# A fused graph layer on one core: x read twice from a host-made layout, edge lists read ready for use, the gate's first layer moved into the main loop, and all 49 key products moved behind the prologue

## The reference

```python
xn = layernorm(x)
# graph attention, 4 heads of 64
h = xn @ W; a_src, a_dst = <h, att_src>, <h, att_dst>
e = leaky_relu(a_src[src] + a_dst[dst], 0.2)
alpha = softmax of e over the edges of each dst
gnn = sigmoid(segment_sum(alpha * h[src], dst) + bias)
# linear attention, 8 heads of 32, with a gate
q, k, v = split(xn @ Wqkv); k = softmax(k, axis=nodes)
out = q @ (k^T v)
hgate = gelu((layernorm(xn) * ln_g + ln_b) @ Wg1 + bg1)
gate = sigmoid(hgate @ Wg2 + bg2)
x = x + gnn + (out * gate) @ Wproj + bproj
# a feed-forward layer on the 3124 nodes with the largest router weight
xn2 = layernorm(x); w = xn2 @ wr + br
x = x + xn2 + (where w is among the top) w * (gelu(xn2 @ w1 + b1) @ w2 + b2)
```

## Time and profile before

| | us |
|---|---|
| median of 3 runs | 1600.1 |
| lowest, highest | 1594.01, 1605.51 |
| span of the profiled execution, first to last instruction | 1323.1 |

### The profile page before, as it was taken

The page is one execution under the profiler, slowest core; times in us unless marked ns, Lnnn a source line. Parts: engine busy times, 40 slices in busy tenths (PEclk is TensorE's granted clock), DMA queues, the critical chain, the costliest instruction groups (busy, mean ns, idle before and its releaser), DMA issues.

```text
span 1323.1 us, 24146 instructions
## 1 busy us (share of the span) xinstructions
PE 1060.3 (80%) x5817; PEld 791.9 (60%) x5817; DVE 1018.3 (77%) x2596; ACT 516.7 (39%) x1155; POOL 854.3 (65%) x891
## 2 busy tenths in 40 slices
PE   5998857785687878878788787897877978779786
PEld 4674635553465566656666566675665766567565
DVE  6776365657788877888788887888878878888788
ACT  4462423212334434343353443434434334344421
POOL 0621656767777777777777777777777777777000
PEclk9999878886788889888898888988889888898889
DMA  9527556766666666666666666666666666665205
GB/s 269 136 72 141 155 184 179 191 178 166 161 173 166 164 160 165 176 158 166 169 162 174 165 161 176 158 171 164 164 173 161 168 164 166 175 164 151 68 1 195
DMA packets 165907, 212.04 MB, mean 160 GB/s; under 512 B 49524, under 2 KB 131252, under 8 KB 165704
## 3 DMA queue, kind: packets, MB, share of 16 engines
q0 software_dynamic: 39984, 110.94, 33.8%
q1 hardware_dynamic: 117570, 97.15, 25.6%
q10 hardware_dynamic: 8306, 3.41, 1.2%
HBM read 165.93 MB, written 45.46 MB: 160 GB/s over the span
## 4 chain that ended last, share of the span: by engine, by line
PE 50%; DVE 15%; issue 11%; ACT 7%; DMA 3%; SPq 1%; DVEq 1%; ACTq 0%; POOL 0%; POOLq 0%
PE bank L1922 15%; PE bank L1887 14%; PE bank L1859 6%; PE bank L1898 5%; ACT L1630 4%; PE bank L1838 3%; DVE hot L1272 2%; PE bank L1847 2%; PE bank L2009 2%; PE bank L1738 2%; DVE ring L1357 2%; DVE xnT L1552 1%; DVE late L1394 1%; DMA parts_d<-wout 1%; ACT bn L1630 1%
## 5 line engine op out<-in xcount | busy, mean ns | idle before, releaser
L774 POOL DMA_INDIRECT ring<-feat_d,idx x832 | 816.0, 981 | 285.8 <-issue 226.5
L1357 DVE TENSOR_TENSOR ring<-ring,bank 128x1024 f32<-128x1024 f32 x208 | 240.0, 1217 | 1.8 <-ACT bank L1620 1.8
L1922 PE MATMUL bank<-late,w_s 128*128 128x256 f32 x768 | 232.4, 463 | 0.4 <-ACT hT L1680 0.4
L1887 PE MATMUL bank<-ring,hot 128*64 128x265 f32 x1664 | 206.8, 401 | 13.3 <-DVE ring L1357 13.2
L1922 PEld LDWEIGHTS bank<-late,w_s 128*128 128x128 f32 x768 | 183.6, 243 | 36.0 <-ACT hT L1680 0.5
L1887 PEld LDWEIGHTS bank<-ring,hot 128*64 128x64 f32 x1664 | 120.0, 141 | 93.8 <-issue 34.2
L1859 PE MATMUL bank<-w_s,hT 128*128 128x256 f32 x720 | 171.0, 392 | 1.2 <-ACT hT L1705 1.2
L1838 PE MATMUL bank<-ident,lk 128*16 128x128 f32 x208 | 42.7, 345 | 161.3 <-DVE lk L1317 161.3
L1620 ACT ACTIVATE bank<-diff 128x64 f32<-128x64 f32 x52 | 11.8, 228 | 376.5 <-DVE diff L1341 362.4
L1859 PEld LDWEIGHTS bank<-w_s,hT 128*128 128x128 f32 x720 | 137.7, 196 | 20.9 <-ACT hT L1705 1.4
L1838 PEld LDWEIGHTS bank<-ident,lk 128*16 128x16 f32 x208 | 17.5, 103 | 177.8 <-DVE lk L1317 136.8
(11 more groups left out here) (284 smaller groups left out, 1611.0 us busy)
## 6 DMA issues: line engine op xcount, KB each, us to landing
parts_d<-zero SPq DMA_DIRECT2D x59, 265.0 KB, 4.0
parts_d<-wout SPq DMA_DIRECT2D x208, 66.2 KB
lists<-dloc_d SPq DMA_DIRECT2D x104, 128.0 KB
ring<-feat_d,idx POOLq DMA_INDIRECT x832
parts<-parts_d SPq DMA_DIRECT2D x49, 265.0 KB
big<-in_x SPq DMA_DIRECT2D x7, 896.0 KB, 11.1
three<-in_x SPq DMA_DIRECT2D x49, 128.0 KB, 3.0
out<-xnT SPq DMA_DIRECT2D x5, 896.0 KB, 4.2
```

Of the source, the lines that this page charges most:

```text
L774: pool.indirect_dma_start(out=ring[:, u * TI + q, 0:AW], out_offset=None, in_=feat_d, in_offset=bass.IndirectOffsetOnAxis(ap=idx[:, u, q:q ...
L1357: V.tensor_tensor(feats, feats, ex[:, g * TG:(g + 1) * TG, :].unsqueeze(3) .to_broadcast([P, TG, HEADS, HD]), ALU.mult).then_inc(S("scaled ...
L1887: mm = T.matmul(bank[2 + n][c * WIN:(c + 1) * WIN, 0:SW], hot[:, q, :], ring[:, u * TI + q, 0:SW], start=(j == 0), stop=(j == TG - 1))
L1922: mm = T.matmul(bank[6 + g][:, m % 2 * 2 * P:(m % 2 + 1) * 2 * P], w1_s[:, t, m * P:(m + 1) * P], xn2T[:, t, :], start=(t == 0), stop=(t = ...
```

## The change

- `x` is laid out by the host as [128, 49, 256], so that a partition's rows are contiguous, and comes in a second time as `xt`, already transposed. ACT's queue loads both (14 DMAs of 7 KB rows), and after them eight edge lists. The transposes of x and their copies are gone.
- The edge lists come in the layouts in which they are used. The list work on POOL, the 48 list transposes and their copies are gone; DVE does six passes of 832 or 1,024 columns over 128 (or 104) partitions.
- The roots are made in four groups (7, 14, 14, 14 tiles).
- The gate's first layer leaves the prologue: `wa_s` has 264 columns; L529, the Gelu of L621, the transposes, their copies and the stores to `hid_d` are gone. In the main loop PE does it a step ahead of the tile's `mixer` (`hidden_ahead`, before `first_sums`), DVE scales it by the root (`scale_hidden`, before `products`), ACT applies Gelu (`gate_hidden`, after `hidden`), and SP loads the root as a row (`load_scales`) in place of `hidT`.
- The target scores are scaled by ACT and no longer by DVE; the products rotate over four banks.
- EARLY goes from 23 to 0: all key products come in the main stretch.
- SP clears ten tiles of `parts_d` after the feature stores and no longer before them.

```diff
-    EARLY = 23
+    EARLY = 0
-WA = C + 2 * HEADS + GH
+WA = C + 2 * HEADS
+        GROUPS = [0, XC, 3 * XC, 5 * XC, NT]
+        prod_bank = lambda i: bank[(2, 3, 6, 7)[i % 4]]
             def _(sp):
...
+                for p in range(PAIRS):
+                    store(p)
...
+                for t in (NT, *range(CLEARED)):
+                    clear(t)
                 for u in range(SLOTS):
                     sp.wait_ge(S(f"feat_out{u}"), 16 * ((PAIRS + SLOTS - 1 - u) // SLOTS))
...
                 def evacuate(i):
-                    products = bank[2 + i % 2]
...
-                    V.tensor_scalar(adst_s[:, i, :], products[:, AW:AW + HEADS], rstd[:, i:i + 1], None, ALU.mult
-                                    ).then_inc(S("adst_made"), 1)
...
-                    V.scalar_tensor_tensor(sc[:, i % 2, 0:GH], products[:, gate_cols], rstd2[:, i:i + 1],
-                                           b1row[:, :], ALU.mult, ALU.add).then_inc(S("hid_asked"), 1)
...
             def _(act):
+                for n in range(7):
+                    part = slice(n * XC, (n + 1) * XC)
+                    act.dma_start(xnT[:, part, :], xt[:, part, :]).then_inc(S(f"x{n}_in"), 16)
+                    act.dma_start(big[:, part, :], x[:, part, :]).then_inc(S(f"x{n}_in"), 16)
+                for o, i in edge_lists:
+                    act.dma_start(o, i).then_inc(S("lists_in"), 16)
...
+                def products(i):
+                    pe.wait_ge(S(f"x{i // XC}_in"), 32)
+                    if i >= 4:
+                        pe.wait_ge(S("adst_made"), i - 3)
...
+                def load_scales(i, u):
+                    if not known_below(i, 2):
+                        sp.wait_ge(S("hidT_made"), i - 1)
+                    sp.dma_start(rrow[:, u, :], rstd_d[bass.ds(i, 1), :].to_broadcast([GH, P])
+                                 ).then_inc(S(f"scales_in{u}"), 16)
...
-                    sp.dma_start(x_pair[p % 5][:, 0:n, 0:C], x.rearrange("(t p) c -> p t c", p=P)[:, 2 * p:2 * p + n, :]
+                    sp.dma_start(x_pair[p % 5][:, 0:n, 0:C], x[:, 2 * p:2 * p + n, :]
...
+                def scale_hidden_from(hid, i, u):
+                    dve.wait_ge(S("hid_done"), i + 1)
+                    dve.wait_ge(S(f"scales_in{u}"), 8 * (i - u) + 16)
+                    V.tensor_tensor(rrow[:, u, :], hid, rrow[:, u, :], ALU.mult).then_inc(S("hid_scaled"), 1)
...
+                def gate_hidden(i, u):
+                    act.wait_ge(S("hid_scaled"), i + 1)
+                    if not known_below(i, 2):
+                        act.wait_ge(S("gate_done"), i - 1)
+                    A.activation(hidT[:, u, :], rrow[:, u, :], ACT.Gelu, bias=b1col[:, 0:1]).then_inc(S("hidT_made"), 1)
...
                 def last_tiles():
                     i = NT - 3
                     merge_exp(i + 1, (i + 1) % 2)
+                    gate_hidden(i + 1, (i + 1) % 2)
+                    gate_hidden(i + 2, i % 2)
                     inverse_root(i, i % 2)
...
+                def hidden_ahead(i, u):
+                    pe.wait_ge(S("sums_kept"), NB * (i + LAG_MERGE - 2) + 1)
+                    if not known_below(i, 1):
+                        pe.wait_ge(S("hid_scaled"), i)
+                    hidden_to(hid_ps[0], i)
...
+                def hidden_to(hid, i):
+                    for t in range(CT):
+                        mm = T.matmul(hid, wg1_s[:, t, :],
+                                      xnT[:, bass.ds(i, 1), t * P:(t + 1) * P].rearrange("p a c -> p (a c)"),
+                                      start=(t == 0), stop=(t == CT - 1))
+                    mm.then_inc(S("hid_done"), 1)
```

More of the change, by code:

```diff
@@ L378, in _ @@
                 for ahead, op in ((1, ALU.is_lt), (2, ALU.is_le)):
-                    then(pool.tensor_tensor(t[:, 0:NG - ahead], first[:, ahead:NG], last[:, 0:NG - ahead], ALU.subtract))
+                    then(pool.tensor_tensor(t[:, 0:NG - ahead], first_e[:, ahead:NG], last_e[:, 0:NG - ahead], ALU.subtract))
                     settle()
@@ L705, in _ @@
-                pe.wait_ge(S("xnT_kept"), TURNED)
-                pe.wait_ge(S("weights_ready"), 4 * CT)
-                def products(i, u):
-                    if i >= 2:
-                        pe.wait_ge(S("hid_asked"), i - 1)
-                    tile = xnT[:, i, :]
+                pe.wait_ge(S("weights_ready"), 2)
+                for t in range(CT):
+                    mm = T.matmul(bank[0][:, 0:WA], ones[:, :], wa_s[:, t, :], start=(t == 0), stop=(t == CT - 1))
+                mm.then_inc(S("columns_summed"), 1)
@@ new lines, in _ @@
+                for t in range(CT):
+                    mm = T.matmul(bank[0][:, 0:GH], ones[:, :], wg1_s[:, t, :], start=(t == 0), stop=(t == CT - 1))
+                mm.then_inc(S("columns_summed"), 1)
+                each(9, 37)
+                pe.wait_ge(S("roots_ready"), len(GROUPS) - 1)
+                pe.wait_ge(S("ident_made"), 1)
+                T.transpose(bank[1][0:NT, 0:P], roots[:, 1, :], ident[:, :]).then_inc(S("rows_turned"), 1)
+                pe.wait_ge(S("bad_asked"), 1)
@@ L1108, in load_node @@
                         sp.wait_ge(S("merged"), free)
-                        sp.wait_ge(S("gate_done"), free)
                     for n in range(2):
@@ L1725, in _ @@
                 sweep(act, EARLY, NT, 1, 0, key_tile)
-                steps(act, [EDGES(exps), MERGE(merge_exp), HALF(hidden), LOAD_MIXER(load_mixer), MAXIMUM(logarithms), CONTEXT(context), EDGES(keep_sums),
+                steps(act, [EDGES(exps), MERGE(merge_exp), HALF(hidden), MERGE(gate_hidden), LOAD_MIXER(load_mixer), MAXIMUM(logarithms), CONTEXT(context), EDGES(keep_sums),
                             SUM(inverse_root), MERGE(gates), TURN(keep_turned)])
@@ L2037, with lay_out, padded @@
 FAR = 1 << 20
+def lay_out(x, src, dst):
+    def padded(a, rows, value):
+        full = np.full((-(-a.shape[0] // rows) * rows, *a.shape[1:]), value, a.dtype)
+        full[:a.shape[0]] = a
+        return full
+    x, src, dst = padded(x, P, 0), padded(src, IE, 0), padded(dst, IE, FAR)
+    tiles = x.reshape(-1, P, CT, P)
+    groups = dst.reshape(-1, GE)
+    after = np.full_like(groups, FAR + 1)
+    after[:, :-1] = groups[:, 1:]
+    by_row = lambda a: a.reshape(-1, GI, P, TG).transpose(2, 0, 1, 3).reshape(P, -1)
+    by_run = lambda a: a.reshape(-1, NB, 2, P, TG).transpose(0, 2, 1, 4, 3)
+    first, last = groups[:, 0], groups[:, -1]
+    base = np.broadcast_to(first.reshape(-1, NB, 2, 1, 1), (first.size // GI, NB, 2, P, TG))
+    runs = by_run(groups).reshape(-1, 2 * GE)
+    f = np.float32
+    return {
+        "x": x.reshape(-1, P, C).transpose(1, 0, 2), "xt": tiles.transpose(3, 0, 2, 1).reshape(P, -1, C),
+        "src": src, "dst": dst, "srct": by_row(src),
+        "curt": by_row(groups).astype(f), "nxtt": by_row(after).astype(f),
+        "curn": groups.reshape(P, -1).astype(f), "nxtn": after.reshape(P, -1).astype(f),
+        "curp": runs.astype(f), "basep": by_run(base).reshape(len(runs), -1, P)[:, :, 0].astype(f),
+        "ends": np.stack([first, last]).astype(f), "first": first[None, :],
+    }
 def kernel(**inputs):
```

529 lines of the change are left out of this document (224 added, 305 removed).

## The result

The changed kernel took 1639.4 us in the median of four runs (1631.7 to 1656.4), the kernel before 1602.8 (1594.0 to 1609.9): a ratio of 1.022 (95% interval 1.016 to 1.028). So it is slower by over 1%. The ratio is taken round by round and leaves out the execution of 1656.4, which ran over 1.5% above the fastest. The forecast was 1594 (1568 to 1612) and no change.

What follows compares the result with a forecast made beforehand. It took PE to bound the prologue and a circle through PE, ACT and DVE the loop, not POOL's gathers. Terms -50 + 22 + 22 - 1 + 1 = -6 gave 1594 us, range 1568 to 1612.

Steps and rivals of the forecast that it cites:

- The base: Whole kernel: sum made against the profiled span of 1323.1 us, with 277 us up to the median carried over unchanged.
- ahead of the first scan -28 forecast: Stretch before the loop: 50 us gained in the prologue, 22 us lost in the key products.
- in the loop +21 forecast: Main loop: +22 us for PE's new records, -1 for x in the context sum, 0 for DVE, ACT and SP.
- Prologue, -50: Before the main stretch: DVE becomes the bound, with 61 us of work from 18 on; main stretch begins at 86.5, not 136.8.
- the sign that I had named for being wrong: Prologue: the prediction is wrong if DVE waits there for ACT's roots or for x.
- the rival with the DMA rate of 263: Prologue bound by its DMAs, 24 MB at 263 GB/s: gain only 38 us, time 1606; chance 0.14.
- Keys, +22: Start of the main stretch: 23 more key products at 0.954 us each, hidden by nothing, +22 us.
- PE in the loop, +22: Each step: four new PE records ahead of the window sums add 0.5 us to the circle in about 45 tiles.
- My rival: Loop: new PE work runs at the lower clock, 1.0 us a step, loop costs 45, time 1617; chance 0.12.
- SP, 0: Loop: one 32 KB load replaces another, asked for a step ahead, so it costs nothing.
- ACT, 0: Loop: the new Gelu and perhaps a table load fit in ACT's idle time before the second copy of sums, 0 us.
- Tail, +1: Last tiles: two Gelus and a load ahead of the Ln, whose slack is 0.55 us, cost +1 us.

Runs made afterwards that it cites:

- half the gathers: Kernel before with every second of 16 gathers a step left out from the third step on: 1331.1, later 1337.2 us; changed kernel with the same cut: 1330.9 us.
- looked at again: The kernel before, unchanged, profiled once more: 1322.8 us, and 1320.6 for the run beside it.
- the kernel with the load at the head: Changed kernel with the load of the scale rows moved from near the end of SP's step to its head: 1616.9 us, ratio 1.010.
- short rows: Kernel before with all 16 gathers of a step fetching rows of 260 bytes instead of 1040 from the third step on: 1581.1 us beside 1600.8.

## Why the prediction was wrong

**The base.** The step that failed is the first one: "277 us less than the median of 1600.1. I make the sum against the span and carry the 277 us over unchanged." A span 1.8 to 2 us short of its own time is what all traces here have. Span against span, 1596.9 to 1320.8, the missing time is 259 us in the 51 steps (25.9 us each against 20.9) and 18 ahead of the first scan (182.5 against 164.4), in the key products. The median and the profile belonged to two paces, and the terms of the sum to the wrong one. At the slow pace the terms came out so: ahead of the first scan -28 forecast and -2 measured, in the loop +21 forecast and +47 measured, behind it +1 and +3. Two terms are known to have failed there: the prologue, and SP's load, which stood at nothing; for the rest of the loop's +47 no run shows the cause.

With half the gathers the number fits, -6 forecast and -6 measured, but that is luck: ahead of the first scan -28 forecast and -8 measured (that stretch is at the slow pace there too), in the loop +21 and -5, behind it +1 and +2.5.

**Where the 37 us are.** By first scan, last scan and end, the mean of four traces of the changed kernel (spans 1632.5 to 1656.5) against the one at 1596.9 of the kernel before; with half the gathers one trace each:

| | before | after, slow pace | before, half gathers | after, half gathers |
|---|---|---|---|---|
| first `forth` scan, us | 182.5 | 180.7 | 184.0 | 175.6 |
| first to last scan | 1322.9 | 1369.9 | 1059.6 | 1054.4 |
| after the last scan | 91.5 | 94.6 | 92.9 | 95.4 |

At the slow pace the whole loss lies between the first and the last scan (the traced executions are 48 us apart, the medians 37).

**Prologue, -50: measured -24** (133.0 to 109.0 at the slow pace; the earlier trace rows has 136.83). The timeline of the changed kernel's prologue (start us, us, engine, line):

```profile
31.16 1.89 ACTq L574 DMA_DIRECT2D srcT<-in_srct  x1
31.76 1.35 PEld L641 LDWEIGHTS bank<-hT,ones 128*128 128x128 f32 x4 [14.97 <-DMA b1col<-in_L_mix_bg]
...
33.08 1.28 ACT L579 ACT_TABLE_LOAD   x1 [33.08 <-issue]
...
99.26 0.49 DVE L470 TENSOR_SCALAR parts<-bank,roots 128x260 f32<-128x260 f32 x1 [0.40 <-PE bank L653]
...
100.44 5.90 SPq L300 DMA_DIRECT2D parts_d<-zero  x9
...
109.03 9.94 PE L1972 MATMUL bank<-hT,xnT 128*128 128x256 f32 x32 [9.81 <-PEq L716]
```

I had ACT's loads done in 10 us, "22 issues of about 0.45 us, 10 us". They took 33: the first ten 0.44 to 0.75 us each, and from the eleventh on about 2 us apiece (31.16). That the queue was full is my reading; no run tests it. So DVE's work began at 34, not 18, and the sign that I had named for being wrong is there, DVE waiting for ACT's roots, 12.8 us the first time:

```profile
DVE roots L450 <- ACT three L579: 14.1, 4, 12.8
```

From there to the last scaling are 65 us, against the 61 that I added up. That is near by luck, since DVE was busy for only 52.5 of them and stood for PE and for stores that had not freed its tiles (7.4 us); the step to the main stretch took 9.3, not 7.5. The main stretch so began at 109.0 and not at 86.5, 16 of these 22.5 us by the late start; the other 4 us of the term are that the kernel before itself began at 133.0 here (134.0 when it was looked at again on the chip of 1321). But moving the list loads away did not win it back: the gate's 64 biases, issued behind x, land at 31.8 here and at 31.6 in that experiment. The bytes came at up to 419 GB/s, better than the 351 of the earlier trace rows, so the rival with the DMA rate of 263 was wrong as well; that a small load behind large ones lands late was what I had left out.

**Keys, +22: measured +23** (133.0 to 178.7 for 26 tiles, 109.0 to 177.4 for 49). The difference was right, and the place too: putting them back brought the first scan 16 us forward. But neither stretch had 0.954 us a product: both also hold POOL's first 22 gathers, and with them the 26 tiles took 19 us more than on the chip of 1321.

**PE in the loop, +22: measured about 0** with half the gathers, and nothing gained without it at the slow pace. The place and the size of the delay were right (0.4 us later in every second step with half the gathers); what I had missed is that the restart step can get shorter by as much. My rival had the clock eat more; it gave some back.

**SP, 0: measured some +12 to +19.** The sentence was "it is asked for a step ahead". It isn't: even with half the gathers the row is asked for 1.6 to 4.5 us before its use, where the load that it replaced (717.47 in the profile of before) had its reader on PE, the gate's products at 732.23, 15 us later. A new reader at the head of DVE's step took the slack of that queue, and where SP issues in fits the slack decides. With half the gathers DVE waited for it three times, 1.9 us in all. This is the term that the slow pace turned from nothing into about half of the loss. The cause of the other half stays open; it lies in the loop (the kernel with the load at the head still takes 1.010 of the kernel before, its keys in the main stretch included).

**ACT, 0: right.** With half the gathers the new table load and the Gelu run from 706.77 to 708.47 in one step and from 727.85 to 729.55 in the next; the first copy of sums follows at once, and the second, which alone starts the Ln, waits 1.7 and 1.4 us for PE. The load begins 0.02 us after the Gelu in the tanh form has ended, and the plain Gelu starts at 708.07, 0.02 us after the load. The Trainium skill (ScalarE: Activation LUTs, What ACT_TABLE_LOAD costs) adds a drain of about 1.38 us to a switch; no run here shows it. The Trainium skill also has the plain form and the tanh form in different sets (ScalarE: Activation LUTs, Table sets: the hidden batching unit), and with a load between the two the trace agrees. **Tail, +1: measured +2.5 to 3.**

## What to carry to other kernels

When a profile's span and the measured median differ by more than a few microseconds, take the profile for another pace and price nothing from it before the two agree; a profile is of one execution on one chip. When an engine starts long after the recorded end of what it waited for, look up whose semaphore it was before blaming the queue that looks slow. Count for every load how long before its use it is issued, ahead of a reader that was moved above all: a load with little slack cost next to nothing while its queue was quick. And a small load that was issued behind megabytes landed behind them.

## What was not expected of the hardware

- On six of seven chips about one in ten of SP's plain instructions takes 0.6 to 0.8 us (203 to 292 of some 2,200 in a trace), PE's semaphores go up as much as 10 us behind the recorded ends, and the kernel takes 1600 instead of 1321 us. With 8 gathers a step in place of 16 nearly all of it is gone from the loop; short rows don't help. The Trainium skill (Perfetto Trace Analysis, DMA Instruction — HWDGE (DVE, Sync)) tells of a wait for the descriptor block that DVE and Sync share, as part of a DMA instruction; here moves between registers, which are none, are slow as well.
- An issue on ACT's queue costs 0.44 to 0.75 us for the first ten loads of 0.9 MB and about 2 us from the eleventh on.
- PE's clock came back some 2 us sooner in a kernel whose PE had 0.5 us more to do in each step; without that work it still did so in 9 restart steps of 16, so the work alone is not the reason.
